# Two-layer transformer block with a recurrent layer: PSUM operands for VectorE, small copies on ScalarE, new order tables

## The reference

```python
def attention(q, k, v, mask):
    scores = jnp.einsum('bhqd,bhkd->bhqk', q, k) / jnp.sqrt(jnp.float32(HD))
    scores = scores * mask - 10000.0 * (1.0 - mask)
    probs = jax.nn.softmax(scores, axis=-1)
    return jnp.einsum('bhqk,bhkd->bhqd', probs, v)
...
def step(s, rkvw):
    r_t, k_t, v_t, w_t = rkvw
    a = k_t[:, :, :, None] * v_t[:, :, None, :]
    out = jnp.einsum('bhk,bhkd->bhd', r_t, u * a + s)
    return (a + w_t[:, :, :, None] * s, out)
...
a4 = att.reshape(b, l, H, S)
m = jnp.mean(a4, axis=-1, keepdims=True)
var = jnp.mean((a4 - m) ** 2, axis=-1, keepdims=True)
att = ((a4 - m) * jax.lax.rsqrt(var + EPS)).reshape(b, l, E) * gn_w + gn_b
x = x + att * g @ Wo.T
```

## Time and profile before

| | |
|---|---|
| time, median of 3 runs | 743.11 us (741.23 to 743.57) |
| the profiled execution | 742.92 us, its span 741.1 us |
| PE busy | 646.6 us, 87% of the span |
| DVE busy | 592.4 us, 80% |
| ACT busy | 574.4 us, 78% |
| POOL busy | 368.8 us, 50% |
| TensorE clock | 1.00 granted in every stretch between 100 and 594 us |

### The profile page before, as it was taken

The page is one execution under the profiler, slowest core; times in us unless marked ns, Lnnn a source line. Parts: engine busy times, 40 slices in busy tenths (PEclk is TensorE's granted clock), DMA queues, the critical chain, the costliest instruction groups (busy, mean ns, idle before and its releaser), DMA issues. The chain is left out here.

```text
span 741.1 us, 16759 instructions
## 1 busy us (share of the span) xinstructions
PE 646.6 (87%) x5585; PEld 542.6 (73%) x5585; DVE 592.4 (80%) x1434; ACT 574.4 (78%) x2002; POOL 368.8 (50%) x537
## 2 busy tenths in 40 slices
PE   5578999999999999999999999999999988787254
PEld 4456787888888888888888888888888878675222
DVE  2476579899998989898989898998999877757541
ACT  2578989798989898989989898989898874743111
POOL 1153454656665656646464646556656454414121
PEclk9689999999999999999999999999999999989655
DMA  8900022221304050505040312223140504040400
GB/s 302 319 34 8 2 69 62 62 68 52 86 18 120 2 136 2 136 1 138 1 124 13 94 44 79 59 65 74 31 106 2 136 1 128 2 128 5 123 8 7
DMA packets 54844, 52.76 MB, mean 71 GB/s; under 512 B 6127, under 2 KB 49511, under 8 KB 54375
## 3 DMA queue, kind: packets, MB, share of 16 engines
q1 hardware_dynamic: 54758, 51.70, 25.0%
HBM read 30.72 MB, written 4.19 MB: 47 GB/s over the span
## 5 line engine op out<-in xcount | busy, mean ns | idle before, releaser
L1067 ACT ACTIVATE SC<-SC,NMX 128x128 f32<-128x128 f32 x512 | 198.8, 394 | 6.8 <-DVE NMX L822 6.5
L1067 ACT ACTIVATION_READ_ACCUMULATOR SC<-SC,NMX 128x1 f32 x512 | 99.1, 194 | 0.0
L557 PE MATMUL PS_T<-CST,SC 128*128 128x128 f32 x512 | 81.3, 283 | 15.8 <-ACT SC L1067 6.4
L822 DVE TENSOR_REDUCE NMX<-SC 128x4 f32<-128x512 f32 x128 | 85.0, 668 | 3.4 <-POOL SC L1239 3.1
L799 DVE TENSOR_TENSOR SC<-PS_S,MASK 128x512 f32<-128x512 f32 x128 | 82.8, 670 | 5.9 <-PE PS_S L539 5.9
L1075 ACT ACTIVATE PT<-PS_T 128x512 f32<-128x512 f32 x128 | 77.0, 601 | 11.2 <-PE PS_T L557 10.2
L557 PEld LDWEIGHTS PS_T<-CST,SC 128*128 128x128 f32 x512 | 59.2, 144 | 30.6 <-ACT SC L1067 16.2
L894 DVE TENSOR_TENSOR_SCAN SS<-W,AJ 128x1024 f32<-128x1024 f32 x32 | 73.2, 2286 | 2.5 <-DVE AJ L887 0.5
L469 PE MATMUL PS_B<-B_LT,W 128*128 128x128 f32 x512 | 67.7, 290 | 7.5 <-ACT B_LT L1023 7.4
L469 PEld LDWEIGHTS PS_B<-B_LT,W 128*128 128x128 f32 x512 | 63.6, 203 | 11.4 <-ACT B_LT L1023 11.0
L1289 POOL TENSOR_TENSOR SS<-SS,KR 128x1024 f32<-128x1024 f32 x16 | 37.8, 2364 | 55.9 <-DVE SS L894 55.9
(11 more groups left out here) (154 smaller groups left out, 1600.0 us busy)
## 6 DMA issues: line engine op xcount, KB each, us to landing
...
```

The costliest lines, as they stand in the source:

```text
L557: last = pe.transpose(PS_T[:, j * T:(j + 1) * T], SC[:, nr(b, a) % 2, g, j, :], ident)
L822: dve.tensor_reduce(NMX[:, nr(b, a) % 2, GH * g:GH * g + GH], SC[:, nr(b, a) % 2, g], AX_X, ALU.max, negate=True)\
L1067: last = act.activation(SC[:, nr(b, a) % 2, g, j, :], SC[:, nr(b, a) % 2, g, j, :], ACT.Exp, bias=NMX[:, nr(b, a) % 2, h:h + 1], accum_out ...
```

## The change

The additions of masks on DVE now read the scores from PSUM: for the three groups of DVE_ADDS a_mask writes its product back to PS_S in place, and a_addmask reads it there. PE therefore waits, before it writes to such a bank again, for the addition (a_dadded) and no longer for the multiplication (scores_read). GM, GV and GY lie in the last columns of PS_D, and d_affine writes to PS_D too. d_norm goes from POOL to DVE. d_own and d_ruk have one instruction each in place of two, with u folded into a matrix USEL that is made once at the start. a_lessmask, d_first_states and the copies to PREV, XN and XM go from POOL to ACT. All five tables are new.

```diff
 SP_ORDER = [
-    ("b_wspread", 0, 3), ("d_store", 0, 5), ("b_vstore", 0, 3), ("a_load", 0, 0), ("b_vspread", 0, 3)]
+    ("b_vspread", 0, 4), ("d_store", 0, 6), ("b_wspread", 0, 3), ("b_vstore", 0, 3), ("a_load", 0, 0)]
 PE_ORDER = [
-    ("a_turn", 0, 0), ("b_mlp1", 1, 3), ("a_prob_turn", (0, 3), 1), ("b_mlp2", 0, 3), ("d_turn", 0, 5),
...
+    ("a_scores", 0, 1), ("a_prob_turn", (1, 1), 3), ("d_own", 0, 5), ("b_low2", 2, 4), ("a_prob_turn", (1, 2), 3),
...
+        GM, GV, GY = (PS_D[:, 512 - n * RH:512 - (n - 1) * RH] for n in (1, 2, 3))
...
+        def scores_read(pe, n, g):
+
+            if n >= 0:
+                b, a = turn_of(n)
+                if (a, g) in DVE_ADDS:
+                    pe.wait_ge(a_dadded, nth(DVE_ADDS, b, (a, g)))
+                else:
+                    pe.wait_ge(a_masked, 4 * n + g + 1)
...
             def a_query(b, a):
...
-                pe.wait_ge(a_masked, 4 * nr(b, a))
+                scores_read(pe, nr(b, a) - 1, 3)
...
-                    last = pe.matmul(PS_D[:, t * (P // RS):(t + 1) * (P // RS)], RK[:, t, :], hsel,
+                    last = pe.matmul(PS_D[:, t * (P // RS):(t + 1) * (P // RS)], RK[:, t, :], USEL[:, t, :],
...
+                masked = PS_S[:, g] if arg in DVE_ADDS else SC[:, nr(b, a) % 2, g]
+                dve.tensor_tensor(masked, PS_S[:, g], over_heads(mask), ALU.mult).then_inc(a_masked, 1)
...
-                dve.tensor_tensor(SC[:, nr(b, a) % 2, g], SC[:, nr(b, a) % 2, g], over_heads(MADD[:, b % 2 if a else 2, :]), ALU.add)\
+                if nr(b, a) > 1:
+                    dve.wait_ge(a_turned, 4 * nr(b, a) + g - 7)
+                dve.tensor_tensor(SC[:, nr(b, a) % 2, g], PS_S[:, g], over_heads(MADD[:, b % 2 if a else 2, :]), ALU.add)\
                     .then_inc(a_dadded, 1)
...
             def d_ruk(b, _):
                 dve.wait_ge(b_kr, b + 1)
-                for k in range(CT):
-                    last = dve.scalar_tensor_tensor(RK[:, k, :], KR[:, 1, k, :], col("u", k), KR[:, 0, k, :],
-                                                    ALU.mult, ALU.mult)
-                last.then_inc(d_rk, 1)
+                dve.tensor_tensor(RK[:, :, :], KR[:, 1], KR[:, 0], ALU.mult).then_inc(d_rk, 1)
...
+                dve.tensor_tensor(heads(CV[:, :]), heads(PS_D[:, C:2 * C]), over_tokens(OW[:, :], RH, RS), ALU.mult)\
+                    .then_inc(d_cv, 1)
...
+            def d_norm(b, _):
+                dve.wait_ge(d_gr, 12 * b + 12)
+                dve.tensor_tensor(heads(O[:, :]), heads(O[:, :]), over_tokens(GY[:, :], RH, RS), ALU.mult)\
+                    .then_inc(d_n, 1)
...
-                dve.scalar_tensor_tensor(YT[:, :, :], YA[:, :, :], 0.5, tiles(G[:, :]), ALU.mult, ALU.mult)\
+                dve.scalar_tensor_tensor(YT[:, :, :], tiles(PS_D[:, C:2 * C]), 0.5, tiles(G[:, :]), ALU.mult, ALU.mult)\
                     .then_inc(d_yt, 1)
...
+                act.activation(PREV[:, b, :, :], tiles(values)[:, :, 0:2], ACT.Copy).then_inc(a_prev, 1)
...
+            def a_lessmask(b, _):
...
+                act.activation(MADD[:, b % 2, :], MASK[:, b, :], ACT.Copy, bias=-10000.0, scale=10000.0)\
+                    .then_inc(a_less, 1)
...
+                    act.activation(XN[:, :, 0:1], PREV[:, b, :, 1:2], ACT.Copy)
...
+                act.activation(AJ[:, :, :, 0:1], S0[:, b, :, :].unsqueeze(3), ACT.Copy).then_inc(d_s0, 1)
...
-                    last = act.activation(YA[:, t, :], PS_D[:, t * T:(t + 1) * T], ACT.Identity,
+                    last = act.activation(PS_D[:, C + t * T:C + (t + 1) * T], PS_D[:, t * T:(t + 1) * T], ACT.Identity,
                                           bias=GNC[:, 1, t:t + 1], scale=GNC[:, 0, t:t + 1])
...
+                act.activation(XM[:, :, 0:1], PREV[:, b, :, 0:1], ACT.Copy)
```

More of the change, by code:

```diff
@@ L79 @@
-    ("b_low1", 0, 3), ("d_val", 0, 5), ("a_prob_turn", (1, 1), 2), ("b_low2", 0, 3), ("a_prob_turn", (1, 2), 2),
-    ("d_own", 0, 4), ("a_enc_turn", 0, 1), ("a_prob_turn", (1, 3), 2), ("b_low2", 2, 3), ("d_read", 0, 4),
-    ("a_pv", 1, 2), ("b_decay1", 0, 3), ("d_oturn", 0, 4), ("b_decay2", 0, 3), ("a_val", 1, 1), ("b_keyrec", 0, 3),
-    ("a_key", 1, 1), ("b_keyrec", 1, 3), ("a_out", 1, 2), ("a_turn", 1, 1), ("b_valgate", 0, 3), ("b_valgate", 1, 3),
-    ("a_prob_turn", (0, 0), 0), ("a_query", 1, 1), ("d_yturn", 0, 4), ("a_prob_turn", (0, 1), 0), ("a_scores", 1, 1),
@@ new lines @@
+    ("d_read", 0, 5), ("b_decay1", 0, 4), ("a_prob_turn", (1, 3), 3), ("d_oturn", 0, 5), ("b_decay2", 0, 4),
+    ("b_keyrec", 0, 4), ("a_enc_turn", 0, 2), ("a_pv", 1, 3), ("a_val", 1, 2), ("a_turn", 1, 2), ("b_keyrec", 1, 4),
+    ("a_out", 1, 3), ("a_key", 1, 2), ("b_valgate", 0, 4), ("b_valgate", 1, 4), ("d_yturn", 0, 5), ("a_query", 1, 2),
+    ("a_prob_turn", (0, 0), 1), ("a_scores", 1, 2), ("b_turn", 0, 3), ("d_out", 0, 5), ("a_prob_turn", (0, 1), 1),
+    ("a_turn", 0, 0), ("b_mlp1", 0, 3), ("b_mlp1", 1, 3), ("a_prob_turn", (0, 2), 1), ("b_mlp2", 0, 3),
@@ L181, in build @@
         RK = sb("RK", [CT, T])
+        USEL = sb("USEL", [CT, P // RS])
         O, OQ = sb("O", [C]), sb("OQ", [C])
```

166 lines of the change are left out of this document (72 added, 94 removed).

## The result

The changed kernel takes 709.47 us (median of 4 runs, 706.85 to 709.58) against 742.17 for the kernel before in the same comparison: a ratio of 0.9555, 95% interval 0.9524 to 0.9585. The forecast was 730.5, and the range ended at 712: the sign was right, the gain is 33 us where 12.6 were forecast. The profiled execution has a span of 707.3 us.

The account below looks back on a forecast made before the run. DVE, with least to spare, was taken to set the turn: 36.3 + 0.6 + 0.8 + 0.2 + 0.4 gave 38.3 us instead of 39.25; minus 0.95 times 13.3 gave 730.5 us, forecast 725 to 737, whole range 712 to 752.

Parts of the forecast that it names:

- the turn: One full turn, between starts of b_wspread: 38.3 us instead of 39.25, minus 0.95, counted 13.3 times.
- 36.3 covered: DVE's busy time in one full turn after the change, from 36.25 plus 0.05 of work.
- 0.6 for dependent pairs: DVE steps that need the step before: gaps in place of overlap at nine pairs and two stats-and-moments pairs, 0.6 us.
- 0.8 before b_sum: DVE waits 0.8 us a turn for the MLP before b_sum: PE's 12.1 us against DVE's 11.3.
- PE's way to b_sum: PE's path from B_N's start through scores, turns and MLP (8.1 us) to b_sum takes 12.1 us.
- A PSUM input costs nothing, and I take nothing: Fifteen DVE operations that now have a PSUM input: no change in time, 0 us.
- the slow write in place: Rival: DVE passes reading and writing one PSUM bank cost 1.5 us more a turn, 750 us; chance 0.07.
- The root wait: DVE's wait for POOL's root before B_N, 0.95 us a turn, goes; the wait before D_N goes too.
- The rest has little of what the change touches, I take nothing there: Loads, first turns and drain, outside the 13.3 turns counted: no gain.
- The rival in which it becomes the bound: ACT's added 1.0 us a turn is not absorbed: turn 40.2, 756 us; chance 0.11.
- all waits close: Rival: on DVE only 36.3 covered and 0.6 of pairs remain: turn 36.9, 712 us; chance 0.14.
- PE's figure is not a floor: PE's 38.10 busy of a 39.24 us turn overstates its work, since modelled ends reach past the next start.

Follow-up runs that it names:

- before_psum_gn: The kernel before, tables and placement untouched, with group norm's GM, GV, GY and d_affine's result in PSUM: 743.0 us, ratio 1.0008.
- before_root_first: The kernel before with one edit in POOL's table, b_root(0) ahead of d_norm, the copy to AJ and MADD: 761.6 us, ratio 1.0258.
- after_norm_pool_psum: The changed kernel with d_norm back on POOL behind b_root(0), GY in PSUM except its last value: 721.5 us, ratio 0.9724.
- tables_old_operands: The changed kernel's tables and placement with all operands back in SBUF, d_ruk and d_own in halves: 743.7 us, ratio 1.0014 to the kernel before.
- after_sbuf_gn: The changed kernel with GM, GV, GY and d_affine's result back in SBUF, masks left in PSUM: 742.5 us, ratio 1.0004 to the kernel before.
- before_dve_plus: The kernel before with one extra DVE product a turn behind d_ruk that nobody waits for: 746.9 us, ratio 1.0073.
- after_dve_plus: The changed kernel with one extra DVE product a turn behind d_ruk that nobody waits for: 707.4 us, ratio 0.9539 to the kernel before.

## Why the prediction was wrong, step by step

The forecast took 12.6 us off the span and 33.8 came off. Two terms of the sum were short by 10.6 us each: the turn (0.95 less forecast, 1.91 measured, eleven times) and what lies outside the eleven turns. A third, the place of operands, was taken at nothing; without it the full turns under the new tables would be longer than before.

**The turn, 38.3 against 37.34.** The forecast was 36.3 covered, 0.6 for dependent pairs, 0.8 before b_sum, 0.2 before b_mixed, 0.4 unnamed. Measured in the turn of the windows row: 35.95 covered, 0.59 for dependent pairs, 0.11 before b_sum, none before b_mixed, 0.69 for all others (0.28 before CV, 0.17 before XK, 0.13 before X, 0.11 before QT). Right were the pairs, and PE's way to b_sum: 12.1 estimated from B_N's start, 12.18 measured (402.94 to 415.12). Wrong was the other side of that comparison: DVE's way there came to 11.3 by the sum of rows and to 12.1 in the trace, so the wait of 0.8 was not there. The sum of slots lets every instruction start 0.08 before the end of the one ahead; at five places the next one starts after it instead (QT 0.11, G 0.10, X 0.13, D_MV 0.10, an addition 0.03), which makes 0.9 with the overlap that is lost. That PE's way came out right is in part luck: its MLP took 7.85 (407.23 to 415.08), not 8.1, and QT ended 1.27 behind B_N's start, not 1.1. Covered time fell by 0.3 because A_N, which the earlier trace rows's turn had at 686 ns beside POOL's bias addition, has 404 now; the prediction had no term for it.

**"A PSUM input costs nothing, and I take nothing".** The first half holds: 188 ns a Newton step, 401 for the gate, 680 for the addition, and before_psum_gn at 1.0008. The rule in "VectorE: DVE Perf Modes" of the Trainium skill, by which each would have cost some 65 ns, isn't borne out. The second half is the step of the mechanism that failed. The prediction used the exclusion for d_shift and didn't ask which other instructions the new order puts beside POOL's, and which of them the change makes immune. The edit counted at nothing is worth 33 us under these tables, 11 of them by the clock: without it the turn would be 40.4, above the one before. The forecast came as near as it did by luck, since it also took Newton steps at 0.19 under the new order without asking what kept them there. Nor was the slow write in place seen: 691 ns against 682 for 512 elements, where the rival had put 0.5 us on each of three passes.

**The root wait.** It went, as forecast (14.6 us to 1.7). But it was not a cost of 0.95 a turn that could be had by itself; before_root_first gained nothing and lost 18 us. Nor does d_norm's place decide about this wait: with d_norm on POOL behind the root, B_N waits 0.12 a turn. What moving d_norm to DVE is worth, 12 us by after_norm_pool_psum, is PE's wait for O and the B_N that no longer meets it.

**"The rest has little of what the change touches, I take nothing there".** This was as large an error as the turn's: 2.3 turns' worth, 2.2 us, was counted outside the eleven turns, and 12.8 came. It is the step that failed in the sum. Fill: every kernel with the new tables has 132 to 135.5 us up to the second b_wspread, every one with the old 141.5 to 149.6, whatever its operands, so it is the order. The first sequences show how (before, then changed; PE's probabilities against V, the keys and queries of the next attention, its QT):

```profile
33.45 1.94 PE L565 MATMUL PS_T<-PT,VP 128*32 128x128 f32 x32
...
35.60 1.95 PE L469 MATMUL PS_S<-A_LT,W 128*128 128x128 f32 x16
...
38.80 0.41 DVE L786 TENSOR_TENSOR QT<-PS_S,COL 128x256 f32<-128x256 f32 x1
```

```profile
32.28 1.10 PE L483 MATMUL PS_S<-A_LT,W 128*128 128x128 f32 x8
...
33.30 1.08 PE L579 MATMUL PS_T<-PT,VP 128*32 128x128 f32 x32
...
35.68 0.42 DVE L802 TENSOR_TENSOR QT<-PS_S,COL 128x256 f32<-128x256 f32 x1
```

The old table had all 16 key and query matmuls behind a_pv; the new one does 8 ahead of it and 8 behind, and QT is 3.1 us earlier. Some 0.9 us of a_pv is the clock (below). Rest, 167.8 before: 165.2 for tables_old_operands, 163.1 for after_sbuf_gn, 162.1 for the changed kernel, 165.4 with d_norm on POOL, but also 164.2 for the new code under the old tables. So tables, code and d_norm's place each have a share, group norm's operands hardly any (1.0). How these two stretches come about in full stays open.

**ScalarE.** The rival in which it becomes the bound (0.11) didn't happen; its 1.0 us was even too much (35.56 covered in all). The copies' durations add up to 1.14 a turn but cover only 0.6, for they overlap their neighbours, and where ACT no longer waits (1.7 us of waits a turn in place of 3.5) other starts overlap the end of the one ahead too, which takes off as much. The rival named "all waits close" (turn 36.9, 712 us) came nearest, at 0.14.

**The bound.** The sum was made on DVE. before_dve_plus shows that this was right for the kernel before, and after_dve_plus that it wasn't for the one after, where PE's 37.17 would have been the better thing to add up: "PE's figure is not a floor" was the sentence that turned away from it.
